# Expert stages in which the last batch's routing shares one block with the experts

## The reference

```python
scores = sigmoid(layernorm(x) @ router_w.T)            # 160 experts
top, index = the 8 largest of scores (+ expert_bias)   # weights = 2.5 * top / (sum(top) + 1e-9)
for each picked expert: y = silu(xn @ w_gate[e].T) @ w_down[e].T    # 128 -> 64 -> 128
x = x + sum over the 8 of weight * y + a shared expert of the same form
```

## Time and profile before

| | |
|---|---|
| Median of three runs | 2839.03 us (2836.64 to 2840.02) |
| Profiled execution, its own time | 2871.99 us |
| Its span, first to last instruction | 2871.3 us |
| Mean granted TensorE clock | 0.789 |
| Busy: PE, DVE, ACT, POOL | 2020.4, 1647.2, 1083.0, 1349.4 us |

### The profile page before, as it was taken

How to read it: one execution, slowest core, us unless ns; L and a number is a source line. 1 busy time by engine, 2 the same in 40 slices (tenths; PEclk the granted TensorE clock), 3 DMA queues, 4 the chain that set the end, 5 groups by cost and what they waited for, 6 DMA issues and landing times. The chain is left out here.

```text
span 2871.3 us, 44772 instructions
## 1 busy us (share of the span) xinstructions
PE 2020.4 (70%) x15403; PEld 1129.8 (39%) x15403; DVE 1647.2 (57%) x4701; ACT 1083.0 (38%) x2067; POOL 1349.4 (47%) x1372
## 2 busy tenths in 40 slices
PE   5898887887883775665887889888888467766000
PEld 3456455455461554541332333333332255545000
DVE  5457585775777231456776778778783533145222
ACT  0263453444541443340545543443444144443000
POOL 0043166566673444553445531641554444355775
PEclk9899989889995887775777877876876589787555
DMA  9200001000034664554131121121100656565221
GB/s 370 96 1 4 1 6 34 23 11 33 20 130 155 192 206 155 180 180 121 28 88 48 46 76 25 53 69 36 49 29 25 250 179 207 176 188 174 70 60 44
DMA packets 132471, 275.63 MB, mean 96 GB/s; under 512 B 29411, under 2 KB 44387, under 8 KB 127891
## 3 DMA queue, kind: packets, MB, share of 16 engines
q1 hardware_dynamic: 99478, 205.60, 21.7%
q0 software_dynamic: 32768, 67.17, 7.7%
HBM read 146.34 MB, written 125.93 MB: 95 GB/s over the span
## 5 line engine op out<-in xcount | busy, mean ns | idle before, releaser
L1473 POOL DMA_INDIRECT slots_in<-g_xs,g_place x512 | 510.1, 996 | 373.0 <-issue 122.7
L2518 ACT ACTIVATE b_pT<-b_psE 128x512 f32<-128x512 f32 (+3 forms) x768 | 325.6, 491 | 449.6 <-PE b_psE L2415 392.6
L2271 DVE TENSOR_REDUCE b_peak<-b_psM 128x1 f32<-128x512 f32 (+3 forms) x768 | 395.1, 551 | 148.6 <-PE b_psM L2403 91.3
L1498 POOL DMA_INDIRECT r_xs<-slots_out,g_place x336 | 333.3, 992 | 237.2 <-ACT b_pT L2518 98.3
L2400 PE MATMUL b_psM<-b_kS,b_qS 72*128 72x512 bf16 (+3 forms) x768 | 290.1, 412 | 60.6 <-DVE b_peak L2271 29.7
L2415 PE MATMUL b_psE<-b_qS,b_kS 75*128 75x512 bf16 (+3 forms) x768 | 250.5, 402 | 45.0 <-ACT b_pT L2518 38.6
L1498 POOL DMA_INDIRECT g_xs<-slots_out,g_place x176 | 173.0, 983 | 126.1 <-issue 48.0
L2060 DVE COPY m_staged_w<-wgd 128x192 f32 x512 | 98.3, 264 | 230.0 <-PE m_psY L2002 165.7
L2427 PE MATMUL b_psV<-b_pT,b_vb 128*32 128x512 f32 (+3 forms) x1536 | 205.8, 616 | 30.8 <-POOL b_pT L2582 29.5
L2060 DVE COPY n_staged_w<-wgd 128x192 f32 x512 | 97.5, 263 | 216.0 <-PE n_psY L2002 118.6
L2400 PEld LDWEIGHTS b_psM<-b_kS,b_qS 72*128 72x128 bf16 x768 | 84.5, 112 | 263.7 <-DVE b_peak L2271 151.6
(11 more groups left out here) (639 smaller groups left out, 4167.9 us busy)
## 6 DMA issues: line engine op xcount, KB each, us to landing
wgd<-in_w_gdT SPq DMA_DIRECT2D x8, 3840.0 KB, 22.7
slots_in<-g_xs SPq DMA_DIRECT2D x26, 1024.0 KB
m_rows<-slots_in SPq DMA_DIRECT2D x104, 256.0 KB
slots_out<-m_y SPq DMA_DIRECT2D x104, 256.0 KB
n_rows<-slots_in SPq DMA_DIRECT2D x104, 256.0 KB
slots_out<-n_y SPq DMA_DIRECT2D x104, 256.0 KB
b_qS<-q_parts SPq DMA_DIRECT2D x48, 192.0 KB
b_kS<-k_parts SPq DMA_DIRECT2D x48, 192.0 KB
```

The lines of the kernel that those rows point to most:

```text
L1473: self.nc.gpsimd.indirect_dma_start(self.G.slots_in[self.h], bass.IndirectOffsetOnAxis(self.G.place[:, TPH * self.h + t, k:k + 1], 0), sel ...
L1498: self.nc.gpsimd.indirect_dma_start(self.rows(i)[:, k, :], None, self.G.slots_out[t // TPH], bass.IndirectOffsetOnAxis(self.G.place[:, t, ...
L2271: nc.vector.reduce_max(to, taking()[:, 0:size], AX.X).then_inc(m_taken, 1)
L2518: nc.scalar.activation(pT[:, e % KEPT, h, q0:HALF], psE[:, j % BANKS, q0:HALF], ACT.Exp, scale=SCALE).then_inc(e_taken, 1)
```

## The change

1. `route` no longer has a block of its own. It returns its part for each engine, and `experts` runs these parts ahead of its own work on each engine, in one block, in `m` and in `n`. Its buffers are cut out of `staged_w`, `G.xs[1]` and a small new one; its PSUM tiles are the experts' own.
2. PE goes from the ranks straight to turning the first group's rows, once the counts are copied. ACT copies the ranks from PSUM to SBUF, so that PSUM comes free; DVE then works from the copy, with the plan, `find_places`, `order_weights` and the first weight copies beside the fixed groups. The owners are turned ahead of group 4 (`OWNERS_TURN`) in one of the experts' PSUM tiles and copied by ACT; POOL waits for the places.
3. The first four groups' rows are loaded ahead of the weight chunks of that block, into a buffer that outlives it.
4. `LEAD` goes from 8 to 12.
5. `SEND_IN_ROUTE` goes from 5 to 10 (four times). The transfers of the last batch are tied to groups from the eighth on: three at first, then three for every two groups.
6. The 46 transfers of an `attn_a` key phase go 2, 3, 6, 7, 7, 7, 7, 7 by tile, in place of 11 and then seven times 5. The pieces of routing work on DVE beside the key tiles are dealt out a little differently, with fewer at the last.

```diff
-LEAD = 8
+LEAD = 12
+OWNERS_TURN = 4
+SMALL = 768
+TIED_FROM = 8
-SEND_A_KEY_TILE, SEND_A_QUERY_TILE, SEND_IN_FFN, SEND_IN_ROUTE = 5, 2, 6, 5
+SEND_A_KEY_TILE = (2, 3, 6, 7, 7, 7, 7, 7)
+SEND_A_QUERY_TILE, SEND_IN_FFN, SEND_IN_ROUTE = 2, 6, 10
...
-    PIECES = ((3, 2, 5), (5, 2, 5), (3, 1, 3), (3, 1, 3), (2, 2, 4)) + 3 * ((5, 3, 6),)
+    PIECES = ((3, 2, 5), (3, 2, 6), (4, 1, 3), (3, 1, 3), (2, 2, 4), (5, 3, 6), (5, 3, 6), (4, 1, 6))
...
                 fold_key_squares(t)
-                if b >= 2 and t == 0:
-                    scatters[(b - 2) // BPH](SEND_IN_FFN)
                 if b >= 2:
-                    scatters[(b - 2) // BPH].of_batch(b - 2)(SEND_A_KEY_TILE)
+                    scatters[(b - 2) // BPH].of_batch(b - 2)(SEND_A_KEY_TILE[t])
...
+def load_rows(G, S, sp, h, i):
+    n = h * HALF_GROUPS + i
+    src = G.slots_in[h].rearrange("(g p j) d -> g p (j d)", p=P, j=TURNS)
+    sp.dma_start(S.rows[:, n % DEEP, :, :].rearrange("p j d -> p (j d)"), src[group_order()[i][0]]).then_inc(S.rows_landed[n % DEEP], 16)
...
+def expert_loads(G, W, S, chunks, first_rows=False):
     def loads(sp):
+        if first_rows:
+            for b in range(BPH):
+                sp.wait_ge(S.scattered[b], 16 * TPB * TOPK)
+            for i in range(DEEP):
+                load_rows(G, S, sp, 0, i)
         for c in chunks:
...
+    def on_scalar(act):
...
+        act.wait_ge(ranked, 1)
+        nc.scalar.activation(probs[:, 0, :, :], ps_lo[:].rearrange("p a (b e) -> p (a b) e", b=2)[:, :, 0:EXPERTS], ACT.Copy).then_inc(rank_taken, 1)
...
+                nc.vector.tensor_tensor(beyond, within, more[:].unsqueeze(1).to_broadcast([P, TPB, EXPERTS]), ALU.is_ge)
...
+            dve.sem_inc(placed, 1)
...
+            dve.sem_inc(ordered, 1)
...
-        psX = m.psum("psX", [P, 2, HALF])
-        psH = m.psum("psH", [P, 2, HALF])
+        psXH = m.psum("psXH", [P, 4, HALF])
+        psX, psH = psXH[:, 0:2, :], psXH[:, 2:4, :]
         psY = m.psum("psY", [P, 2, 2, HALF])
+        small = m.sbuf("small", [P, SMALL])
+        C = Carved(staged_w[:].rearrange("p a g i -> p (a g i)"), G.xs[1][:].rearrange("p t d -> p (t d)"), small[:])
+        R = route(nc, m, C, G, W, b // BPH, TPB * (b % BPH), TPB, xn, psY[:].rearrange("p a b n -> p (a b) n"), psXH, xn_free, scatter, loads)
...
                 for n in range(0, count, transfers):
-                    done = min(n // transfers * groups, HALF_GROUPS)
-                    if done:
-                        pool.wait_ge(y_ready, first + done)
+                    done = min(first + n // transfers * groups, (first // HALF_GROUPS + 1) * HALF_GROUPS)
+                    if n:
+                        pool.wait_ge(y_ready, done)
                     issue(min(transfers, count - n))

-            spaced(scatter, TPH * TOPK - scatter.sent, 0, 3, 2)
+            R.on_gpsimd(pool)
+            pool.wait_ge(R.placed, 1)
+            scatter.of_batch(b)
+            spaced(scatter, TPH * TOPK - scatter.sent, TIED_FROM, 3, 2)
+            pool.wait_ge(R.ordered, 1)
...
                 pe.wait_ge(rows_landed[n % DEEP], 16 * (n // DEEP + 1))
                 if n >= 2:
                     pe.wait_ge(xT_ready, n - 1)
+                elif n == 0:
+                    pe.wait_ge(R.counts_taken, 1)
+                if n == OWNERS_TURN:
+                    pe.wait_ge(R.owner_ready, 1)
+                    for i in range(OWNERS):
+                        last = nc.tensor.matmul(psX[0:1, n % 2, i * P:(i + 1) * P], R.owner[:, i:i + 1], G.ident[:], start=True, stop=True)
+                    last.then_inc(R.owner_turned, 1)
+                    pe.wait_ge(R.owner_taken, 1)
...
                 if n >= 2:
                     pe.wait_ge(hT_ready, n - 1)
+                else:
+                    pe.wait_ge(R.shared_taken, 2)
...
                 if n >= 2:
                     pe.wait_ge(y_ready, n - 1)
+                else:
+                    pe.wait_ge(R.rank_taken, 1)
...
+            R.on_tensor(pe)
...
+                if n == OWNERS_TURN:
+                    act.wait_ge(R.owner_turned, 1)
+                    nc.scalar.activation(G.tile_expert[0:1, b // BPH, :], psX[0:1, n % 2, 0:DYN_TILES], ACT.Copy).then_inc(R.owner_taken, 1)
...
+            R.on_scalar(act)
...
+            R.on_vector(dve)
             for c in range(CHUNKS):
                 dve.wait_ge(S.weights_landed[c], 16)
             for d in range(DYN_GROUPS):
                 stage_weights(0, d)
+            dve.wait_ge(R.owner_taken, 1)
```

More of the change, by code:

```diff
@@ L1 @@
 import itertools
+import math
 from contextlib import ExitStack
@@ L1543, in expert_loads, with route @@
     return loads
-def route(nc, stage, G, W, h, first, tiles, xn, xn_free=None, send=None, loads=None):
+def route(nc, m, C, G, W, h, first, tiles, xn, ps_lo, ps_hi, xn_free, send, loads):
     WINDOWS = tiles // TPB
@@ L1892, in experts @@
-def experts(nc, stage, G, S, scatter, out=None):
-    with Memory(nc, stage) as m:
-        rows = m.sbuf("rows", [P, DEEP, TURNS, DM])
+    here = slice(TPH * h + first, TPH * h + first + tiles)
+    x = G.x[:].rearrange("p b t d -> p (b t) d")[:, here, :]
+    w8, place = G.w8[:, here, :], G.place[:, here, :]
+    freed = C.sbuf("freed", [P, 2 * tiles * P])
+    xnT = freed[:, 0:tiles * P]
+    hs = freed[0:INTER, tiles * P:].rearrange("p (u n) -> p u n", n=HALF)
+    beyond = freed[:, 0:TPB * EXPERTS].rearrange("p (t e) -> p t e", e=EXPERTS)
@@ new lines, in route @@
+    more = C.sbuf("more", [P, EXPERTS]) if resumed else None
+    ends = C.sbuf("ends", [P, 2, EXPERTS])
+    share = C.sbuf("share", [1, EXPERTS], BF16)
+    owner, older = m.sbuf("owner", [P, OWNERS]), C.sbuf("older", [P, OWNERS])
+    keys = C.sbuf("keys", [P, TPB, TOPK])
+    key_i, expert_i, slot_i, low = (C.sbuf(n, [P, TPB, TOPK], I32) for n in ("key_i", "expert_i", "slot_i", "low"))
+    router_landed, shared_landed = m.sem("router_landed"), m.sem("shared_landed")
+    made, share_ready, xn_ready, turned, xnT_ready, logits_done, logits_taken, probs_ready, picked_ready, counted = (m.sem(n) for n in (
+        "made", "share_ready", "xn_ready", "turned", "xnT_ready", "logits_done", "logits_taken", "probs_ready", "picked_ready",
+        "counted"))
@@ new lines, in on_tensor, with turn, score, shared @@
+    def on_tensor(pe):
+        def turn():
+            for u in range(CHUNKS_X):
+                pe.wait_ge(xn_ready, u + 1)
+                for t in range(4):
+                    last = nc.tensor.transpose(ps_lo[:, u, t * P:(t + 1) * P], xn[:, 4 * u + t, :], G.ident[:])
+                last.then_inc(turned, 1)
+        def score(w):
+            to = (ps_hi if w == 0 else ps_lo)[:].rearrange("p a (b e) -> p (a b) e", b=2)
+            pe.wait_ge(xnT_ready, 2 + 2 * w if w == 0 else CHUNKS_X)
+            for t in range(TPB):
+                last = nc.tensor.matmul(to[:, t, 0:EXPERTS], xnT[:, (w * TPB + t) * P:(w * TPB + t + 1) * P], wr[:],
+                                        start=True, stop=True)
+            last.then_inc(logits_done, 1)
+        def shared(u):
+            if u:
+                pe.wait_ge(hs_ready, u)
+            nc.tensor.matmul(ps_hi[0:INTER, 1, :], wgs[:], xnT[:, u * HALF:(u + 1) * HALF], start=True, stop=True).then_inc(up_shared, 1)
+            pe.wait_ge(hs_ready, u + 1)
+            if u >= 2:
+                pe.wait_ge(shared_taken, u - 1)
+            for t in range(4):
+                last = nc.tensor.matmul(ps_hi[:, 2 + u % 2, t * DM:(t + 1) * DM], hs[:, u % HS, t * P:(t + 1) * P], wds[:],
+                                        start=True, stop=True)
+            last.then_inc(shared_done, 1)
+        def total_counts():
+            pe.wait_ge(picked_ready, WINDOWS)
+            nc.tensor.matmul(ps_hi[:, 0, 0:EXPERTS], ones_bf[:], before[:, tiles, :], start=True, stop=True).then_inc(counted, 1)
+        def ranks(w):
+            pe.wait_ge(share_ready, 1)
+            to = ps_lo[:].rearrange("p a (b e) -> p (a b) e", b=2)
+            if w:
+                pe.wait_ge(rank_taken, 1)
+            for t in range(TPB):
+                nc.tensor.matmul(to[:, t, 0:EXPERTS], earlier[:], picked[:, w * TPB + t, :], start=True, stop=False)
+                nc.tensor.matmul(to[:, t, 0:EXPERTS], ones_bf[:], before[:, w * TPB + t, :], start=False, stop=False)
+                last = nc.tensor.matmul(to[:, t, 0:EXPERTS], ones_bf[0:1, :], share[:], start=False, stop=True)
+            last.then_inc(ranked, 1)
+        pe.wait_ge(made, 3)
+        pe.wait_ge(router_landed, 32)
+        turn()
+        for w in range(WINDOWS):
+            score(w)
+        pe.wait_ge(shared_landed, 32)
+        pe.wait_ge(logits_taken, 1)
+        for u in range(CHUNKS_X):
+            shared(u)
+        total_counts()
+        ranks(0)
@@ L1898, in experts @@
+def experts(nc, stage, G, W, S, b, xn, xn_free, scatter, loads, out=None):
+    with Memory(nc, stage) as m:
+        rows, rows_landed = S.rows, S.rows_landed
```

(6 more changed lines are left out.)

586 lines of the change are left out of this document (257 added, 329 removed).

## The result

| | before | changed |
|---|---|---|
| Median | 2839.53 us (2836.64 to 2850.87, 4 runs) | 2871.74 us (2865.47 to 2881.59, 4 runs) |
| Ratio | | 1.0098, 95% interval 1.0076 to 1.012 |
| Span profiled, clock | 2871.3 us, 0.789 | 2865.3 us, 0.798 |

The change made the kernel 1% slower; 2788 us was forecast. In the changed file line 1476 is the sending (1473 before), 1501 the gathering (1498), 1551 the loads of rows (1920), 2018, 2033 and 2046 turn, up and down (1978, 1991, 2002), 2071, 2077 and 2083 ACT's xT, silu and y, and 1743 the last loop of `choose` (1736).

A forecast was written before the change was run, and what follows sets the result against it. It took waits and short-step chains where expert halves start to bound the kernel, no engine being full. Terms -21.4, -8.3, -16.2 and -5 sum to -50.9: profiled 2871.99 to 2821.1, less 33 to the median, 2788 us; range 2772 to 2808.

The forecast's parts named there:

- Start of m, -21.4: First half's start in m: first up matmul at 907.5, not 930.98, less 2.1 us for the owners; bounds -18 and -24.
- Twenty more transfers stand in the routing, from about 905 on 25 us of POOL: Rival on sends in m's routing: last batch's transfers come late, n's middle gets some 6 us wait; 2802 us, chance 0.14.
- Start of n, -16.2: First half's start in n: group 4's load waits behind the weights, turn 4 at 2299.4, not 2315.62; bounds -10 and -22.
- near 18: Sign in n's start: four turns by 2292, a gap, then turn 4 near 18 us after the ranks' end.
- Middle of m, -8.3: Between m's halves: last transfers fit before the last store, so loads need not wait for them; bounds -6 and -9.
- Middle of n: Between n's halves: no scatter is waited for, so 0 us change.
- `LEAD` 12 is priced at nothing: Experts' first groups in m: twelve fixed groups lead, flexible group 0 has 16 us spare; cost 0.
- gathering falls behind: Rival, second halves: adds start some 12 us later, POOL waits an estimated 8 for buffers; if not made up 2796, chance 0.10.
- The clock: Rival, experts: clock falls as PE's rests go; at 0.72 the time is 2858; sign clearly under 0.8; chance 0.05.
- Key phases, -5: Key phases of batches 2 and 3: fewer transfers ahead of the second fold, -2.5 us each; bounds 0 and -4.4 each.
- the other dealing of pieces leaves the same work on DVE: Key phases: dealing the routing pieces differently was given no gain or cost; batch 1 gets nothing.
- the low bounds: Best case of all terms together, summed in the prediction as -64.8 us, giving 2774 us.

The follow-up runs named there:

- e4: The kernel before with 10 transfers in each portion of the routing, not 5, nothing else changed: ratio 1.0036 to before.
- e5: The changed kernel with LEAD 8, 5 transfers per routing portion, key tiles 11 then 5 each, three for two groups tied from group 2: 0.9944 of before.
- e15: The changed kernel with LEAD 8, short rows of transfers, twos and ones by group, and the key phase's old pieces: 0.985 of before.
- e12: The changed kernel, unchanged, run again on the chip of e13 to e15: 1.0118 of before.
- e13: The changed kernel with LEAD 8 in place of 12, same chip as e12: 0.9961 of before.
- e14: The changed kernel, LEAD 12 kept, with the first gathered rows added after flexible group 5's weights, not 8's: 0.9955 of before.
- e6: The kernel before with key-phase transfers 2, 3, 6, 7, 7, 7, 7, 7 by tile, its pieces unchanged: 1.0027 of before.
- e1: The kernel before, unchanged, run again for a profile: ratio 1.001; 2861 us on this chip.
- e3: The changed kernel with LEAD 8 in place of 12: 0.9944 of before.
- e8: As e5, but transfers tied two and one for each group in turn, not three for two groups: 0.9929 of before.
- e9: As e8, but with the key phase's old pieces, on a chip where before took 2662 us: 0.9862 of before.
- e11: As e9, but 8 transfers in each portion of batch 3's feed-forward block, not 6: 0.9873 of before.
- e16: As e15, but with LEAD 12 and e14's earlier first add, where before ran at 2662.03 us: 0.9854 of before.
- e17: The changed kernel, unchanged, on a chip where before ran at 2662.03 us: 0.987 of before.
- e7: The changed kernel with LEAD 8, last batch's transfers in the experts only signalled, not sent (result incomplete): 2752.85 us, one run.

## Why the prediction was wrong

- **Start of m, -21.4:** the mechanism was right. ACT's copy took 1.24 us and the first up came 1.8 us after the last rank; the owners' round, costed at 2.1 us, took PE 1.1 (0.6 at line 2014 and a wait of 0.47). The failed step stands elsewhere: "Twenty more transfers stand in the routing, from about 905 on 25 us of POOL". I counted POOL's time alone, and asked only whether the later sends would be late. The transfers stand beside the eight searches ahead of the ranks, and stretch these: 20 us in m and 17 in n (e4). To the first up -3.8 and -6.2 us are left. In m ACT's first silu then waits 7.6 us beside the next ten sends, and group 4 is turned 17.3 us after the ranks, 12.3 in e5.
- **Start of n, -16.2:** the load of group 4 that waits behind the weights did not occur in the changed kernel, since the stretched routing gave the weights time to land, 2.1 us before the ranks' end. Where the routing is short it did, as the prediction has it: in e5 and e15 the last chunk lands 15.3 and 15.5 us after the ranks, and turn 4 comes at 17.5 and 17.6 us, where the prediction has "near 18".
- **Middle of m, -8.3:** right; from last y to next turn 12.1 us became 4.1. Middle of n: right, no new wait.
- **"`LEAD` 12 is priced at nothing":** the second failed step. Against LEAD 8 on the same chip it costs 31.2 and 23.1 us in the second halves (e12 and e13). The rival "gathering falls behind" had the cause (the wait for buffers, 24 us measured in m where I estimated 8), but not its price: nothing of it stood at the end (215.2 us from the last y, 217.3 before), and it is the making up, in rows of twelve, beside which the groups slow down. That moving the add alone takes the loss away is shown (e14); that the rows of twelve are the way is read from the timeline.
- **The clock,** my rival for a slower kernel, has a part. Over the whole run 0.798 was granted against 0.789, but in the second halves it is 0.76 and 0.74, under the 0.8 that I named as a sign (0.78 and 0.80 before; windows 1088.7 to 1285.2 and 2443 to 2650.1 us, before 1103.2 to 1287.8 and 2468.6 to 2654). PE's busy time grew by 8.9 of 21.7 us in n, which is the most that the clock can have cost there, and by 2.3 of 11.9 in m. PE idles more in these halves, and e14's edit took that loss away, so the fall looks like a consequence; that was not tested by itself.
- **Key phases, -5:** the two profiles have batch 2 at 5.5 us less and batch 3 at 8.1 more. The new sends alone bring the folds no closer (e6), and "the other dealing of pieces leaves the same work on DVE" missed some 7 to 10 us in batch 3, most of it DVE's wait for later matmuls of PE (e5 against e15).
- **The same error under all three:** that what POOL issues is free for others while POOL has time. The trace of before had the rows to see it by. In n there is no send from 2306.3 to 2315.9 us, and four groups take 2.7 us each though the clock is low (0.60), where m's average is 3.1. At 2315.6, 2317.6, 2321.8 and 2323.7 us the next groups are turned: 2.0 us apart without a send, 4.2 with three beside them, and 2.0 again. I used both paces and did not ask for the difference.
- **The sum:** the low bounds -24, -9, -22 and -8.8 add up to -63.8, not -64.8, so the low end was 2775. That decides nothing.

From 2788 to the 2871.7 measured are 84 us. An estimate from the runs: 46 for the late add (e12 less e14), 37 for the stretched routing (e4) and 8 for the key phases (the two profiles), less 17 that the first halves gain by the transfers moved ahead of them (e4 against e1), in all 74. The runs are from several chips, and the remaining 10 are not assigned. The two profiles themselves cannot be used for it: they differ by 6 us the other way, and 9.7 of that is `layer_b`, which the change leaves alone (944.7 us for 954.4). It ranges from 939.3 (e3) to 954.4 over the runs of one kind; why was not settled.

## What to carry to other kernels

Price an indirect transfer of GpSimd by what it does to the engines beside it, not by GpSimd's free time: compare the pace of the same work with and without transfers in the trace. Keep rows of them short and away from chains of many small instructions, and make sure that no wait turns an even stream into bursts; here moving one add forward was worth 1.6% on one kind of chip, and nothing on the other. When a lead is lengthened, look at everything that is counted from it.

## What the runs showed of the hardware

- The chips are of two kinds here: those of e1 to e8 and e12 to e15, where before takes 2841 to 2861 us (2840 at the changed kernel's first measurement), and those of e9 to e11 and of e16 and e17, where it takes 2662. What sets them apart was not settled.
- On the first kind a transfer of GpSimd beside the experts cost them 0.68 us (e7). In a long row DVE issued one short instruction each 1.4 us, from about the sixteenth transfer on in the routing; in the second half a row of twelve was enough to leave ACT idle for 13.6 us and PE for 11.2. On the second kind a row of 25 cost nothing in the routing (e17).
- The gaps have no releaser in the profile, and outlast the weights' load (49 GB/s at 906 to 914 us), so bandwidth is not it. That the instructions themselves arrive late was my reading, and the trace speaks against it: from 886 to 931 us, around DVE's gaps in m's routing, the changed kernel's DMA trace has 368 packets on the hardware queue and 1046 on the software queue, and none on the two queues of kind "instruction" (124 and 101 packets in the whole run).
- The cause of the gaps inside the chip stays open.
- The changed kernel is 1.0 to 1.2% slower than before on the first kind and 1.3% faster on the second. The version of e15 beats both on the first (0.985); on the second, as e9, it beats before (0.9862) and cannot be told from the changed kernel (0.987).
